# Unread f16 products on TensorE around the first and last steps of each stage of a two-layer adaLN kernel

## The chip, the cores and the metric

The program runs on one core of one Trainium2 chip. The metric is the device time of one execution in microseconds (us); the median of three runs of the kernel before is 1408.56 us. TensorE (PE in the profile, PEld for its weight loads), VectorE (DVE), ScalarE (ACT), GpSimd (POOL) and SyncE (SP, which issues the transfers) run side by side and meet at semaphores. TensorE's clock has two levels, 2.4 GHz (granted clock 1.00 in the profile) and 1.2 GHz (0.50).

## The reference

Two transformer layers over x of 32 batches x 256 tokens x 128 channels, each with a modulation computed from a condition. What is computed, cut down:

```python
mod = (_silu(L0_c) @ L0_wmod).reshape(32, 6, 1, -1)          # shifts, scales, gates
h = _layernorm(x) * (1 + ca) + sa
x = x + ga * attn0(h)      # 16 heads of 8; q, k l2-normalized; tanh resonance; sigmoid gates
h = _layernorm(x) * (1 + cb) + sb
x = x + gb * experts0(h)   # each expert picks the token with the largest logit in a group of 32
mod = (_silu(L1_c) @ L1_wmod).reshape(32, 6, 1, -1)
h = _layernorm(x) * (1 + ca) + sa
x = x + ga * attn1(h)      # 16 heads of 8; rope; softmax
h = _layernorm(x) * (1 + cb) + sb
x = x + gb * ffn1(h)       # silu(h W1) * (h W2), then two 512x512 layers with gelu, then W3
```

## The kernel before

All of x stays in SBUF. The program is a row of stages, each one an `nc.Block()` in which every engine has its own list of instructions: the set-up (line 96), attention of layer 0 (line 275), the experts (lines 779 and 932), the set-up of layer 1 (line 2254), attention of layer 1 (line 2824, which takes `attention_1_bounded` when the scores are small, as here), a short weight test `ffn_1_setup` (line 2700) and the feed-forward part `ffn_1` (line 2851). At the end of a block each engine executes a DRAIN and adds one to a gather semaphore; GpSimd collects these and sets a release semaphore, and only then does any engine enter the next block.

Inside a block the order is written out by hand. Both attention stages run `step(b, p)` for b from -3 to 32 (`every`): in four `pair`s of a step TensorE computes the scores of batch b (`scores`, line 384 or 1961) and the sums over its values (`heads`, 397 or 1975), and between them prepares the batches to come: `turn` (transposes of batch b+3, line 319 or 1913), `project_qk` (327 or 1921), `project_logits_v` (335 and 339) or `project_v` (1928), `turn_keys` and `turn_queries` (349, 359, or 1938, 1947). In steps -3 to -1 there are no scores yet, so a step is a chain: VectorE and GpSimd normalize, TensorE turns, VectorE copies, TensorE projects, and so on. ScalarE computes the exponentials or tanh of the scores (lines 473, 2046) into `probs`.

The experts stage works on chunks of 8 batches: TensorE turns (`turn`, 970), scores (978), sends tokens to slots, multiplies with the experts' matrices and hands the results back; its last work is `hand_back` (1047), after which VectorE and GpSimd add to x.

The weight test is one product (line 2704) of the largest rounding loss, read by VectorE for a flag that selects the branch of the feed-forward part. In `ffn_1` TensorE turns tile 0 (2401), then `gates(0, m)` for m = 0 to 3 (pairs of high and low parts, line 2390), `turn(1)`, and then `step(n)`, a dense stream of products of 128x512 on line 2390.

PSUM has 8 banks of 512 columns; `SC` are the four banks of the scores, `ident16` is a 128x128 unit matrix in f16 that the set-up loads.

## Time and profile before

| | us |
|---|---|
| median of 3 runs | 1408.56 (1406.98 to 1411.34) |
| the profiled execution, its own time | 1414.56 |
| its span, first to last instruction | 1412.6 |
| TensorE busy | 1258.7 (89%) |
| VectorE busy | 1066.8 (76%) |
| ScalarE busy | 926.0 (66%) |
| mean granted TensorE clock | 0.919 |

The stages in the span, by the views of the profile: set-up to 20.9 us, attention 0 to 416.1, experts to 687.4, set-up of layer 1 to 690, attention 1 to 1041.7, weight test to 1043.3, feed-forward to the end. The profile's second part cuts the span into 40 slices and gives for each the busy share of each engine and the granted clock in tenths. The timeline gives start, duration, engine, line, what is written and read, and in brackets how long the engine sat idle before and what released it.

### The profile page before, as it was taken

What the parts mean: (1) busy time and instruction counts of PE and PEld (TensorE: products, weight loads), DVE (VectorE), ACT (ScalarE), POOL (GpSimd) and SP (SyncE); (2) the same over time, 40 slices, a digit from 0 to 9 for tenths busy, and PEclk for the clock granted to TensorE, in tenths of its full rate; (3) what the DMA queues carried; (4) which work ended last, traced back from release to release, by engine and by line L of the source; (5) the groups of instructions that cost most, each with busy time, mean ns of one, the idle gap of its engine ahead of it and who ended that gap; (6) DMA issues with size and microseconds to landing.
All of it is one profiled execution on the core that took longest, in us unless ns stands there. A gap on an engine that the chain in (4) does not pass through costs nothing. (4 is left out here: it accounts for less than half of the span.)

```text
span 1412.6 us, 39634 instructions
## 1 busy us (share of the span) xinstructions
PE 1258.7 (89%) x13658; PEld 845.9 (60%) x13658; DVE 1066.8 (76%) x2966; ACT 926.0 (66%) x1280; POOL 538.4 (38%) x743
## 2 busy tenths in 40 slices
PE   2699999999977798896589999999858999999998
PEld 1455555555534677776355555555426877777876
DVE  2799999999945675743589999999835777777763
ACT  0498888888962443432078888888736666667675
POOL 1244443333412131210333343433525566566553
PEclk7599999999995897976689999999978999999999
DMA  3411111111002011100200000000000000000000
GB/s 84 154 36 35 33 35 40 36 33 33 23 10 56 23 27 27 33 2 17 91 13 13 15 11 15 13 13 15 9 2 1 9 15 15 7 15 15 7 15 24
DMA packets 44748, 37.78 MB, mean 27 GB/s; under 512 B 5008, under 2 KB 43472, under 8 KB 44144
## 3 DMA queue, kind: packets, MB, share of 16 engines
q1 hardware_dynamic: 44656, 36.56, 9.2%
q8 instruction: 57, 0.93, 0.3%
q14 instruction: 35, 0.29, 0.1%
HBM read 32.21 MB, written 4.34 MB: 26 GB/s over the span
## 5 line engine op out<-in xcount | busy, mean ns | idle before, releaser
L2046 ACT ACTIVATE a_probs<-psum_all 128x1024 f32<-128x1024 f32 x256 | 248.2, 1023 | 85.8 <-PE psum_all L1961 85.8
L473 ACT ACTIVATE probs<-psum_all,biases 128x1024 f32<-128x1024 f32 x256 | 272.7, 1113 | 39.0 <-PE psum_all L384 37.6
L2390 PE MATMUL psum_all<-ffn_hi,weights_r 128*128 128x512 f32 x704 | 285.7, 406 | 8.6 <-POOL ffn_lo L2350 5.3
L2390 PE MATMUL psum_all<-ffn_lo,weights_r 128*128 128x512 f32 x704 | 279.4, 397 | 0.0
L2350 POOL TENSOR_TENSOR ffn_lo<-ffn_full,ffn_hi 128x512 fp32r<-128x512 f32 x144 | 188.8, 1319 | 126.4 <-ACT ffn_hi L2475 86.7
L2390 PEld LDWEIGHTS psum_all<-ffn_hi,weights_r 128*128 128x128 f32 x704 | 134.1, 190 | 50.2 <-DVE ffn_full L2605 9.6
L2390 PEld LDWEIGHTS psum_all<-ffn_lo,weights_r 128*128 128x128 f32 x704 | 134.4, 191 | 26.8
L397 PE MATMUL psum_all<-probs,vpad 128*32 128x257 f32 x2048 | 139.1, 389 | 0.7 <-ACT probs L473 0.3
L1975 PE MATMUL psum_all<-a_probs,vpad 128*32 128x256 f32 x2048 | 137.8, 387 | 1.2 <-DVE a_sums L2197 1.2
L2487 ACT ACTIVATE ffn_full<-psum_all,scales 128x512 f32<-128x512 f32 x128 | 88.3, 690 | 68.5 <-PE psum_all L2390 68.3
L2350 DVE TENSOR_TENSOR ffn_lo<-ffn_full,ffn_hi 128x512 fp32r<-128x512 f32 x64 | 55.2, 863 | 79.9 <-ACT ffn_hi L2490 79.9
L496 POOL TENSOR_TENSOR a_vareps<-a_moments,eps 128x2 f32<-128x2 f32 x64 | 15.1, 236 | 201.0 <-DVE a_moments L555 201.0
L2490 ACT ACTIVATE ffn_hi<-psum_all,scales 128x512 fp32r<-128x512 f32 x128 | 87.4, 683 | 0.0
L397 PEld LDWEIGHTS psum_all<-probs,vpad 128*32 128x32 f32 x2048 | 53.7, 109 | 51.8 <-issue 21.4
L384 PE MATMUL psum_all<-a_qT,a_kT 32*128 32x256 f16 x1024 | 77.2, 276 | 8.0 <-ACT probs L473 6.3
L1975 PEld LDWEIGHTS psum_all<-a_probs,vpad 128*32 128x32 f32 x2048 | 53.6, 109 | 50.9 <-issue 27.1
L2067 POOL TENSOR_TENSOR a_vareps<-a_moments,eps 128x2 f32<-128x2 f32 x32 | 6.3, 197 | 176.6 <-DVE a_moments L2116 176.6
L1961 PE MATMUL psum_all<-a_qT,a_kT 32*128 32x256 f16 x1024 | 65.6, 276 | 4.1 <-ACT a_probs L2046 2.2
L1113 ACT COPY e_slots<-psum_all 128x512 f32<-128x512 f32 x64 | 34.4, 589 | 50.8 <-PE psum_all L992 50.7
L2475 ACT CAST ffn_hi<-ffn_full 128x512 fp32r<-128x512 f32 x64 | 39.7, 620 | 42.8 <-DVE ffn_full L2605 42.8
L1022 PE MATMUL psum_all<-e_relued,f 32*128 32x64 f32 x1024 | 50.7, 373 | 17.5 <-issue 10.6
L1151 POOL TENSOR_TENSOR X<-X,e_delta 128x256 f32<-128x256 f32 x32 | 23.6, 736 | 106.6 <-DVE e_delta L1224 106.3
(220 smaller groups left out, 2693.7 us busy)
## 6 DMA issues: line engine op xcount, KB each, us to landing
a_mod_gate<-modulation_table SPq DMA_DIRECT2D x64, 128.0 KB, 2.9
a_mod_norm<-modulation_table SPq DMA_DIRECT2D x32, 128.0 KB, 3.0
X<-in_x SPq DMA_DIRECT2D x32, 128.0 KB, 2.9
f<-in_f SPq DMA_DIRECT2D x2, 2048.0 KB, 9.8
e_mod_norm<-modulation_table SPq DMA_DIRECT2D x32, 128.0 KB, 2.9
out<-X SPq DMA_DIRECT2D x16, 256.0 KB, 2.3
e_gates<-modulation_table SPq DMA_DIRECT2D x32, 64.0 KB, 2.9
weights<-in_h SPq DMA_DIRECT2D x2, 1024.0 KB, 7.3
```

The costliest lines, as they stand in the source:

```text
L384: last = nc.tensor.matmul(SC[c % 2][:, (TT * r + kb) * T:(TT * r + kb + 1) * T], kT[p][rows, g, kb * P:(kb + 1) * P], qT[p][rows, g, :], s ...
L397: last = nc.tensor.matmul(PO[32 * r:32 * r + 32, :], vpad[p][:, kb, G * r + g, :], probs[:, (2 * g + r // 2) % 4, r % 2, kb, 0:UNIT], star ...
L473: nc.scalar.activation(probs[:, c % 4, :, :, 0:T].rearrange("p r k q -> p (r k) q"), SC[c % 2].rearrange("p (a q) -> p a q", q=T), ACT.Tan ...
L1022: last = nc.tensor.matmul(B_SLOTS[s][:, e * CG:(e + 1) * CG], f2[rows, r * EB + e, :], relued[r][rows, e, :], start=True, stop=True)
L1961: last = nc.tensor.matmul(SC[c % 2][:, (TT * r + kb) * T:(TT * r + kb + 1) * T], kT[p][rows, g, kb * P:(kb + 1) * P], qT[p][rows, g, :], s ...
L1975: last = nc.tensor.matmul(PO[32 * r:32 * r + 32, s * T:(s + 1) * T], vpad[p][:, kb, G * r + g, :], probs[:, (2 * g + r // 2) % 4, r % 2, k ...
L2046: nc.scalar.activation(probs[:, c % 4, :, :, :].rearrange("p r k q -> p (r k q)"), SC[c % 2], ACT.Exp, scale=float(np.float32(1.0) / np.sq ...
L2350: subtract(lo[layer][:, k, :], full[layer][:, k, :], hi[layer][:, k, :].bitcast(F32), ALU.subtract).then_inc(done[layer], 1)
L2390: ins = nc.tensor.matmul(dst, weights[:, w0:w0 + P], part[layer][:, k, :], start=first and i == 0, stop=last and i == len(parts) - 1)
L2475: nc.scalar.copy(hi[1][:, k, :], full[1][:, k, :]).then_inc(hi_done[1], 1)
L2487: nc.scalar.activation(full[layer + 1][:, m, :], bank[m % 2], ACT.Gelu, scale=scales[:, 1 + layer, m:m + 1]).then_inc(full_done[layer + 1], 1)
L2490: nc.scalar.activation(hi[layer + 1][:, m, :], bank[m % 2], ACT.Gelu, scale=scales[:, 1 + layer, m:m + 1]).then_inc(hi_done[layer + 1], 1)
```

## The change

A new function issues products that nobody reads, and it is called in front of, between and behind the first and last steps of the stages. The stationary operand is `ident16`, the moving one the same matrix four times, so each product streams 512 columns in f16 and writes one bank.

```diff
+def keep_busy(nc, dst, ident16, n):
+    for _ in range(n):
+        nc.tensor.matmul(dst, ident16[:, :], ident16[:, :].unsqueeze(1).broadcast_to([P, dst.shape[1] // P, P]), start=True, stop=True)
...
 # attention 0
+            def spare(b, pair):
+                places = {(-3, 3): 4, (-2, 0): 18, (-2, 3): 4, (-1, 0): 2, (-1, 1): 4, (-1, 2): 8, (B, 3): 24}
+                return places.get((b, pair), 0) if isinstance(b, int) else 0
...
                         if there(b + 3):
                             turn(b + 3)
+                    keep_busy(nc, SC[0][:, 0:512], ident16, spare(b, pair))
+            keep_busy(nc, SC[0][:, 0:512], ident16, 24)
             pe.wait_ge(wg_done, 2)
             every(pe, step)
...
 # experts, behind the last step
+            wait(pe, sent_done, B)
+            keep_busy(nc, bank[4], sbuf["ident16"], 36)
...
 # attention 1 (bounded)
+            places = {(-3, 3): 3, (-2, 0): 10, (-2, 3): 10, (-1, 1): 2, (-1, 2): 10, (B, 3): 20}
...
+                keep_busy(nc, SC[0][:, 0:512], ident16, spare(b, pair))
...
 # feed-forward
         turn(0)
+        keep_busy(nc, bank[0], sbuf["ident16"], 12)
         for m in range(KH):
             gates(0, m)
+            keep_busy(nc, bank[0], sbuf["ident16"], 2)
         turn(1)
+        keep_busy(nc, bank[0], sbuf["ident16"], 4)
...
 # weight test
             nc.tensor.matmul(psum[0:1, 0:P], worst[:, :], ident[:, :], start=True, stop=True).then_inc(moved, 1)
+            keep_busy(nc, psum[:, 512:1024], sbuf["ident16"], 16)
```

Executed are 88 such products in attention 0, 36 in the experts stage, 55 in attention 1, 16 in the weight test and 24 in the feed-forward part, 219 in all. The code inside the loops is untouched, and so are the lists of the other engines.

TensorE at the start of attention 0, before (L319 `turn`, L327 `project_qk`, L335 the logits, L339 the values, L349 `turn_keys`):

```order
L309 UNCONDITIONAL_BRANCH
L319 MATMUL psum_all<-ident,a_h 128x128 x2
L319 MATMUL psum_all<-ident,a_xn 128x128 x2
L327 MATMUL psum_all<-wqk,a_xnT 128x256 x2
L335 MATMUL psum_all<-a_wg,a_xnT 128x32 x2
```

and after (all line numbers are larger by 7):

```order
L316 UNCONDITIONAL_BRANCH
L62 MATMUL psum_all<-ident 128x512 x24
L326 MATMUL psum_all<-ident,a_h 128x128 x2
L326 MATMUL psum_all<-ident,a_xn 128x128 x2
L62 MATMUL psum_all<-ident 128x512 x4
L334 MATMUL psum_all<-wqk,a_xnT 128x256 x2
L342 MATMUL psum_all<-a_wg,a_xnT 128x32 x2
L62 MATMUL psum_all<-ident 128x512 x18
```

Nothing is moved: 24 products stand in front of the first turn, 4 between turn and projection, 18 between the first batch's logits and the second batch's turn.

TensorE at the end of attention 0 and the start of the experts, before (L397 `heads`, L408 `project_out`, L970 the experts' first turn):

```order
L408 MATMUL psum_all<-a_wo_gated,a_oT 128x128 x2
L397 MATMUL psum_all<-probs,vpad 32x257 x8
L408 MATMUL psum_all<-a_wo_gated,a_oT 128x128 x2
L275 UNCONDITIONAL_BRANCH
L957 UNCONDITIONAL_BRANCH
L970 MATMUL psum_all<-ident,e_h 128x128 x2
```

and after:

```order
L415 MATMUL psum_all<-a_wo_gated,a_oT 128x128 x2
L404 MATMUL psum_all<-probs,vpad 32x257 x8
L415 MATMUL psum_all<-a_wo_gated,a_oT 128x128 x2
L62 MATMUL psum_all<-ident 128x512 x24
L282 UNCONDITIONAL_BRANCH
L971 UNCONDITIONAL_BRANCH
L984 MATMUL psum_all<-ident,e_h 128x128 x2
```

The 24 products stand ahead of the branch that leaves the block, so ahead of the block's DRAIN. In the same way 36 stand behind the experts' last `hand_back`, 20 behind the last `project_out` of attention 1, and 16 behind the product of the weight test:

```order
L2729 MATMUL psum_all<-ident,s_worst 1x128
L62 MATMUL psum_all<-ident 128x512 x16
L2725 UNCONDITIONAL_BRANCH
L2882 UNCONDITIONAL_BRANCH
L2788 TENSOR_LOAD exact_weights
```

where before the branch followed the product of line 2704 at once.

## Rows read from the trace of the kernel before

**Rows 1.** The page's part 2, granted clock in tenths, 40 slices of 35.3 us.

```profile
PEclk7599999999995897976689999999978999999999
```

**Rows 2.** Windows: stretch, length, each engine's busy us, granted clock, DMA share, GB/s.

```profile
15.80:63.60 47.80, 20.73 (x116) 14.40 (x120) 28.39 (x118) 8.32 (x14) 13.42 (x24) 0.50 0.37 129
...
415.40:418.60 3.20, 0.06 (x1) 0.00 (x0) 1.15 (x6) 0.00 (x0) 0.86 (x2) 1.00 0.09 25
418.60:421.10 2.50, 0.00 (x0) 0.00 (x1) 1.35 (x5) 0.00 (x0) 0.04 (x1) 0.50 0.13 39
...
688.30:715.50 27.20, 12.65 (x58) 8.51 (x58) 17.48 (x51) 1.94 (x2) 8.92 (x20) 0.50 0.33 118
...
1063.80:1066.90 3.10, 0.83 (x4) 0.40 (x3) 3.03 (x6) 1.90 (x2) 1.42 (x2) 1.00 0.00 0
```

**Rows 3.** Timeline of TensorE in the lead-in of attention 0.

```profile
41.40 0.66 PE L319 MATMUL psum_all<-ident,a_h 128*128 128x128 f32 x2 [5.54 <-DVE a_xn L561]
...
43.46 2.07 PE L327 MATMUL psum_all<-wqk,a_xnT 128*128 128x256 f32 x4 [0.97 <-DVE a_xnT L597]
...
46.04 1.20 PE L339 MATMUL psum_all<-wv,a_hT 128*128 128x128 f32 x4
...
68.95 1.13 PE L327 MATMUL psum_all<-wqk,a_xnT 128*128 128x256 f32 x4
...
70.28 0.69 PE L339 MATMUL psum_all<-wv,a_hT 128*128 128x128 f32 x4
```

**Rows 4.** Timeline, products of 512 columns back to back, at either clock.

```profile
1068.86 0.63 PE L2390 MATMUL psum_all<-ffn_lo,weights_r 128*128 128x512 f32 x1
1069.29 0.63 PE L2390 MATMUL psum_all<-ffn_hi,weights_r 128*128 128x512 f32 x1
...
1086.91 0.39 PE L2390 MATMUL psum_all<-ffn_hi,weights_r 128*128 128x512 f32 x1
1087.14 0.39 PE L2390 MATMUL psum_all<-ffn_lo,weights_r 128*128 128x512 f32 x1
```

**Rows 5.** Source view, line 275 (end of attention 0): duration ns, start.

```profile
L275 PEldq DRAIN  x1: 753/753/753, 414.8 to 414.8; - x1
L275 DVEq DRAIN  x1: 459/459/459, 415.5 to 415.5; - x1
```

**Rows 6.** Timeline, the first product of the experts stage.

```profile
421.13 0.66 PE L970 MATMUL psum_all<-ident,e_h 128*128 128x128 f32 x2 [5.67 <-DVE e_h L1195]
```

**Rows 7.** Source view, line 932 (end of the experts).

```profile
L932 PEldq DRAIN  x1: 637/637/637, 685.3 to 685.3; - x1
...
L932 POOLq DRAIN  x1: 826/826/826, 686.5 to 686.5; - x1
```

**Rows 8.** Timeline, the last products of attention 1.

```profile
1037.61 0.71 PE L2001 MATMUL psum_all<-a_wo_gated,a_oT 128*128 128x128 f32 x4 [0.46 <-ACT a_oT L2040]
```

**Rows 9.** Source view, line 2824 (end of attention 1).

```profile
L2824 PEldq DRAIN  x1: 68/68/68, 1041.5 to 1041.5; - x1
```

**Rows 10.** Source view, line 2700 (end of the weight test).

```profile
L2700 PEldq DRAIN  x1: 633/633/633, 1042.1 to 1042.1; - x1
L2700 DVEq DRAIN  x1: 156/156/156, 1043.0 to 1043.0; - x1
```

**Rows 11.** Timeline of TensorE, lead-in of attention 1.

```profile
693.88 0.69 PE L1913 MATMUL psum_all<-ident,a_xhat 128*128 128x128 f32 x2 [7.96 <-DVE a_xhat L2124]
...
699.92 0.69 PE L1913 MATMUL psum_all<-ident,a_xhat 128*128 128x128 f32 x2 [2.64 <-DVE a_xhat L2124]
...
703.14 2.07 PE L1921 MATMUL psum_all<-wqk,a_hT 128*128 128x256 f32 x4 [2.53 <-DVE a_hT L2133]
```

**Rows 12.** The chain that ended last, start of the feed-forward part.

```profile
1048.08 1.13 PE psum_all L2401 x4
...
1052.18 2.06 PE psum_all L2390 x4
...
1066.83 7.81 PE psum_all L2390 x26
```

More of the change, by code:

```diff
@@ L2002, in project_out, with spare @@
             last.then_inc(projected, 1)
+        def spare(b, pair):
+            places = {(-3, 3): 3, (-2, 0): 10, (-2, 3): 10, (-1, 1): 2, (-1, 2): 10, (B, 3): 20}
+            return places.get((b, pair), 0) if isinstance(b, int) else 0
         def step(b, p):
```

## The prediction

> **What bounds the kernel now.** I read the clock first. The page grants 2.4 GHz nearly everywhere, but not at the start, in the experts stage and around the seams between stages [rows 1]; the windows give exact stretches at 0.50: 15.8 to 63.6 us and 688.3 to 715.5, the lead-ins of the two attention stages, and from 418.6 on, where the experts begin [rows 2]. What precedes the fall is idle time: TensorE ended its work in attention 0 at 415.5 [rows 5], and between 418.6 and 421.1 the clock is at 0.50 without any product in between [rows 2]. Even 2 us are enough: between 1063.8 and 1066.9 it was busy for 0.83 us, with 1.00 granted [rows 2], and the products behind it, at 1069, run at half speed again [rows 4].
>
> Then I asked what ends last in such a lead-in. It is a chain that goes round all engines: TensorE waits 5.54 us for VectorE at 41.4, 0.97 us at 43.5 [rows 3]. So a faster TensorE shortens the chain only by its own links, and unread products fit only into its waits. From 63.6 to 415.4 and in the dense part of the feed-forward stage nothing changes.
>
> Last the seams. The DRAIN that ends each engine's block spans the time until its last instruction is finished: TensorE's at the end of attention 0 took 753 ns, from 414.8 to 415.5, beside the 0.7 us of the last projection, and VectorE's ended at 416.0 [rows 5]. TensorE's was 637 ns at the end of the experts [rows 7] and 633 ns behind the one product of the weight test [rows 10]. The whole core enters the next block only after the last DRAIN. That is what decides this case, since four of the added groups stand ahead of a DRAIN.
>
> **Price of one product.** No f16 product of 512 columns is in the trace. The nearest are those of line 2390 with 512 columns: 0.43 us from start to start at the low clock, 0.23 at the high one [rows 4]. I take these. Those are products of a wider type that reload their weights each time, so an f16 one can hardly be slower; as bounds I allow half of the price at the high clock and 0.43 throughout.
>
> The Trainium skill ("TensorE: Matmul & The Clock Gate", Back-to-back issue gap) gives about 131 ns per product of 512 columns in a sustained stream of weight loads and products. The rows show 230 ns for such pairs; by the page the groups at the seams would be cheap, a rival below.
>
> **The seams, which cost.** Each end is compared with the engine that was last.
> - End of attention 0: 24 x 0.23 = 5.5 us behind 415.5 gives 421.0; VectorE was done at 416.0 [rows 5]. +5.0. The clock is high there [rows 2].
> - End of the experts: 36 x 0.23 = 8.3 behind 686.0 gives 694.3; GpSimd was last, at 687.3 [rows 7]. +6.9 at the high clock. In the last third of the experts the clock swings [rows 1]; at the low one until it rises 8 to 16 products cost 0.2 more each, +8.5 to +10.
> - End of attention 1: the last projection ended at 1038.3 [rows 8], yet TensorE's DRAIN came at 1041.5 [rows 9], so over 3 us pass in the jump across the other branch's code. 20 x 0.23 = 4.6 behind 1038.3 gives 1042.9. If the jump overlaps them, +1.4; if it begins after them, +4.6. The instructions are issued ahead of their execution (the DRAIN of the weight test starts with its product, at 1042.1 [rows 10]), so I take nearer the lower end: +2.0.
> - Weight test: 16 x 0.23 = 3.7 behind 1042.7 gives 1046.4, VectorE was done at 1043.2 [rows 10]. +3.2; at the low clock, which is possible after the gap in the seam before, +6.6.
>
> Sum: 5.0 + 6.9 + 2.0 + 3.2 = +17.1 us, from 16.5 (the jump overlapped) to 26.
>
> Do they buy the next stage a high clock? No. What follows the release is again idle TensorE: the experts' first turn came at 421.1 [rows 6], 5.1 us after VectorE's DRAIN; attention 1's at 693.9 [rows 11], 6.6 after GpSimd's; the feed-forward's at 1048.1 [rows 12], 4.9 after VectorE's. These distances stay, because the chain starts at the release. The clock fell after 3.1 us at most [rows 2, 5], so each stage starts at 0.50 as before, and the groups at the seams are pure cost.
>
> **The lead-ins, which gain.**
> - Attention 0. The 24 products in front start at the block's entry, 20.9 us: at most 24 x 0.43 = 10.3, so done by 31.2, when the first turn begins, and earlier since such a dense run raises the clock (products at line 2390 went from 0.43 to 0.23 in the same way). The 18 cost 4.1 at the high clock and 7.7 at the low, against a wait of 5.54; the groups of 4 take 0.92 against a wait of 0.97 [rows 3], and those of 2, 4 and 8 behind the second batch stand in like waits. With the clock up, projection, logits and values take 68.95 to 70.97 instead of 43.46 to 47.24 [rows 3]: 1.8 us less for the second batch and for the third, 1.1 for the first, which has no values. Three turns save 0.45 each (half their streaming), and the first scores and sums until 63.6 another 1.2. Sum 7.2 us. VectorE is busy for 28.4 of the 47.8 us there [rows 2] and is next in the chain when TensorE is early; I let it take back a third: -4.9 (from -7 to +1, if the clock falls again in the wait before the turn and the 18 run slow).
> - Attention 1. The stage starts at 0.50. 3 slow products behind the first turn cost 1.3 us, 0.5 over their wait; the 10 behind the projection fit into 2.64 us only once the clock is up, the next 10 into 2.53 [rows 11]; VectorE has about 2 us of other work before it needs that turn. From the second projection on the clock is up: 2.07 becomes 1.13 and 1.06 becomes 0.69 (as the like products in [rows 3]), with the wait between them twice 1.1 us, and 0.7 for turns and scores; against it 0.3 for the 3. Sum -2.6 (from -3.5 to 0).
> - Feed-forward. Idle before the first turn, so 12 products at 0.50: 5.2 us in a wait of 3.0 (from 1049.2 to 1052.2) [rows 12], +2.2 if the clock stays down, +1.3 if it rises on the way; then the first gates take about 1.1 instead of 2.06, -0.9. The middle is a chain of ScalarE and VectorE, in which the groups of 2 and 4 hide. The dense part began at the low clock, 26 products in 7.81 us [rows 12] instead of 26 x 0.23 = 6.0, -1.7 if it now begins high. Sum -0.9 at best, +1.5 at worst; I take -0.6.
>
> **Sum.** +17.1 - 4.9 - 2.6 - 0.6 = +9.0 us. On the profiled execution, span 1412.6, that is a span of 1421.6 (its own time 1414.56 would be 1423.6); on the median of the runs, 1408.56, it is **1417.6**.
>
> **Rivals.**
> - The seams don't hold: a DRAIN lets the products run on behind it. Then the groups at the seams cost nothing, they fill the waits up to the next first turn almost exactly (5.7 us of idle against 5.5 [rows 6]; 7.96 against 8.3 [rows 11]), and every stage starts at the high clock. Against it: three DRAINs that ended with their last product [rows 5, 7, 10]. The 17.1 go, the experts' first steps gain perhaps 2, attention 1 and the feed-forward another 2: 1408.56 - 8.1 - 4 = 1396.5. Chance 0.08. This is the faster side.
> - The products are cheap, about 0.13 us, near the page's rate and half that of [rows 4]. Seams 2.6 + 3.4 + 0 + 1.6 = 7.6, lead-ins -8.1: 1408. The condition is that the narrow type streams at half the distance of [rows 4]; for it stands nothing in the trace, where 512 columns take the same 0.23 in every pair. Chance 0.04. Beside it: the lead-ins give their full 7 + 3.5 + 1 and the jump overlaps: +16.5 - 11.5 = +5 and less, 1409 to 1412.8. Chance 0.09.
> - The lead-ins gain nothing, because the waits that are left between the groups let the clock fall again and slow products then overrun their waits: +17.1 + 0 to 2, 1425.7 to 1428. Its place is the wait that is left of some 2 us between the 24 or the 18 and the next turn; 2 us sufficed once [rows 2]. Chance 0.08.
> - The experts end, or the weight test begins, at the low clock: 3.4 more for one, up to 7 for both, 1421 to 1425. Chance 0.13.
>
> **How the numbers follow.** Forecast 0.58 (1413 to 1421), rivals 0.08, 0.13, 0.08, 0.13. The range 1410.5 to 1427 leaves out the faster rival and the outermost of two others. A measurement of this kernel can tell about 0.3%, 4.2 us, from no change: faster 0.08, same 0.13, slower 0.79.
>
> **What would show it.** TensorE's DRAIN at the four seams long (5.5, 8.3, over 1 and 3.7 us) and last; the distance from a release to a stage's first turn unchanged; the clock at 0.50 at the experts' and at attention 1's first turn, but at 1.00 from about 28 us on in the lead-in of attention 0; the first tanh of line 473 some 3 us earlier within its stage, and that of the fifth some 5. I am wrong if VectorE starts the experts' statistics at 417 while TensorE still runs the 24, or if the unread products stand less than 0.2 us apart.

## The result, and the profile after

The changed kernel takes 1425.09 us (median of 14 runs, 1421.82 to 1429.8), the kernel before, beside it, 1410.96 us (14 runs, 1403.31 to 1421.27). The ratio is 1.0086 (95%: 1.0067 to 1.0105), which on 1410.96 is 12.1 us slower, from 9.5 to 14.8; the medians are 14.1 apart. The profiled execution has a span of 1422.3 us, against 1412.6. The forecast was 1417.6 us in a range of 1410.5 to 1427, slower. The direction and the range held, and so did the mechanism at the ends of the stages; what the forecast said of the feed-forward part and of the experts did not. The forecast itself was 7.5 us under the median, and 2.4 of that lie in the kernel before, whose median was 1410.96 in these runs and not 1408.56. In the experiments below three runs of the kernel before took 1861 to 3798 us; the ratios leave them out, and its medians move by at most 0.5 us with them.

First the ends of the stages. Source views of the lines of the four blocks in the profile after (engine, duration in ns, start in us):

```profile
L282 DVEq DRAIN  x1: 459/459/459, 410.1 to 410.1; - x1
L282 PEldq DRAIN  x1: 4050/4050/4050, 411.2 to 411.2; - x1
...
L946 POOLq DRAIN  x1: 826/826/826, 686.7 to 686.7; - x1
L946 PEldq DRAIN  x1: 4048/4048/4048, 690.0 to 690.0; - x1
...
L2850 DVEq DRAIN  x1: 54/54/54, 1045.8 to 1045.8; - x1
L2850 PEldq DRAIN  x1: 502/502/502, 1046.7 to 1046.7; - x1
...
L2725 DVEq DRAIN  x1: 156/156/156, 1048.4 to 1048.4; - x1
L2725 PEldq DRAIN  x1: 1907/1907/1907, 1049.7 to 1049.7; - x1
```

In [rows 5, 7, 10] TensorE's DRAIN took 0.6 to 0.75 us and was over before VectorE's or GpSimd's. Now it is the last one in each of the four blocks (at the end of attention 1 it was the last before too, by 0.2 us). The timeline of TensorE shows what it waits for (start, duration, operation, in brackets the idle time before):

```profile
409.30 0.71 PE L415 MATMUL psum_all<-a_wo_gated,a_oT 128*128 128x128 f32 x4 [0.61 <-DVE a_oT L723]
409.85 5.34 PE L62 MATMUL psum_all<-ident 128*128 128x512 f16 x24
420.36 0.66 PE L984 MATMUL psum_all<-ident,e_h 128*128 128x128 f32 x2 [5.16 <-DVE e_h L1211]
...
686.05 7.94 PE L62 MATMUL psum_all<-ident 128*128 128x512 f16 x36
700.57 0.69 PE L1929 MATMUL psum_all<-ident,a_xhat 128*128 128x128 f32 x2 [6.57 <-DVE a_xhat L2146]
...
1042.66 4.48 PE L62 MATMUL psum_all<-ident 128*128 128x512 f16 x20
...
1047.97 3.63 PE L62 MATMUL psum_all<-ident 128*128 128x512 f16 x16
1056.52 1.12 PE L2423 MATMUL psum_all<-ident,ffn_xhat 128*128 128x128 f32 x4 [4.92 <-DVE ffn_xhat L2601]
```

The DRAIN at 411.2 ends at 415.2, and so do the 24 products (409.85 + 5.34 = 415.2). The next stage's first turn comes 5.15 us behind that, as it came 5.1 us behind VectorE's DRAIN in [rows 5, 6]. The same holds at attention 1 (6.55 us, as in [rows 7, 11]) and in the feed-forward part (4.90, as in [rows 10, 12]). The products delay the release, and what follows the release stays as it was, the idle TensorE with it.

The clock, by windows (stretch, length, busy us of PE, PEld, DVE, ACT and POOL with counts, granted clock, DMA share, GB/s):

```profile
30.30:33.60 3.30, 3.30 (x10) 2.10 (x8) 1.51 (x7) 0.00 (x0) 0.90 (x2) 0.50 0.00 0
23.60:30.10 6.50, 3.58 (x19) 1.58 (x17) 2.18 (x12) 0.00 (x0) 3.26 (x6) 1.00 0.34 100
...
415.50:418.90 3.40, 0.00 (x0) 0.00 (x0) 0.73 (x5) 0.00 (x0) 0.90 (x2) 1.00 0.13 39
419.40:421.50 2.10, 0.68 (x3) 0.31 (x3) 1.42 (x8) 0.37 (x1) 0.32 (x2) 0.50 0.21 62
699.28:706.11 6.83, 5.54 (x14) 2.98 (x15) 3.58 (x11) 0.00 (x0) 2.55 (x4) 0.50 0.91 317
...
1074.80:1081.50 6.70, 5.95 (x14) 4.72 (x15) 2.05 (x11) 3.10 (x5) 4.35 (x5) 0.50 0.00 0
```

In the lead-in of attention 0 the clock is at 1.00 from 23.6 us on, but for 3.4 us about 32, where it was at 0.50 until 63.6 [rows 2]. It is still at 1.00 right behind the seam (415.5 to 418.9, TensorE idle) and at 0.50 when the experts' first turn comes. In attention 1 it is at 0.50 for 6.8 us in place of 27 [rows 2]. In the feed-forward part it fell again at the start of the dense stream (last row).

### The profile page after: what moved, and what is told of

Read it like the earlier page. It is cut to its first block and busy times, and to the rows that moved or that the text cites. A ratio compares the mean times of both kernels' runs of the same rounds, so it can differ in the third digit from the quotient of the medians.

```text
span 1422.3 us, 40072 instructions
## 1 busy us (share of the span) xinstructions
PE 1285.7 (90%) x13877; PEld 849.9 (60%) x13877; DVE 1067.6 (75%) x2966; ACT 926.0 (65%) x1280; POOL 538.6 (38%) x743
## 5 line engine op out<-in xcount | busy, mean ns | idle before, releaser
L62 PE MATMUL psum_all<-ident 128*128 128x512 f16 x219 | 57.1, 413 | 7.3 <-PEq L103 7.3
## 6 DMA issues: line engine op xcount, KB each, us to landing
f<-in_f SPq DMA_DIRECT2D x2, 2048.0 KB, 10.5
```

The costliest lines, as they stand in the source:

```text
L62: nc.tensor.matmul(dst, ident16[:, :], ident16[:, :].unsqueeze(1).broadcast_to([P, dst.shape[1] // P, P]), start=True, stop=True)
```

## Where the time went, stage by stage

Each stage can be cut at its DRAINs, since they stand in every profile: a stage runs from the release to the DRAIN of the engine that was last before (VectorE's, in the experts stage GpSimd's), a seam from there to the next release. Worked out in this way from the start and the duration of the DRAINs in the two traces, in us:

| part | before | after | change | forecast |
|---|---|---|---|---|
| attention 0, entry to VectorE's DRAIN | 395.2 | 391.1 | -4.2 | -4.9 |
| seam behind it | 0.56 | 5.25 | +4.7 | +5.0 |
| experts | 270.8 | 271.8 | +1.0 | 0 |
| seam, with the set-up of layer 1 | 2.8 | 9.3 | +6.5 | +6.9 |
| attention 1, release to VectorE's DRAIN | 351.2 | 349.0 | -2.2 | -2.6 |
| seam behind it | 0.5 | 1.6 | +1.1 | +2.0 |
| weight test | 1.35 | 4.2 | +2.9 | +3.2 |
| feed-forward | 369.2 | 370.4 | +1.2 | -0.6 |

With 1.3 us less in the set-up, which the change doesn't touch, these make the 9.7 us between the two spans. How steady such a length is, the profiles of the experiments below show: attention 0 took 394.2 to 395.3 us in four kernels without its lead-in products and 390.0 to 391.1 in nine with them, attention 1 351.2 to 352.9 in four without (one more left out, below) and 349.0 to 352.0 in nine with them. The experts stage is not steady: the same code took 263.0 to 274.1 us in nine profiles. This is why the experiments are read by stages, and by medians where the experts stage is meant.

## Experiments

**1. The seams and the lead-ins apart.** Two kernels, each with one half of the change.

```diff
 # lead-ins alone (lead_only), against the changed kernel
-                places = {..., (-1, 2): 8, (B, 3): 24}
+                places = {..., (-1, 2): 8, (B, 3): 0}
...
-            wait(pe, sent_done, B)
-            keep_busy(nc, bank[4], sbuf["ident16"], 36)
...
-            places = {..., (-1, 2): 10, (B, 3): 20}
+            places = {..., (-1, 2): 10, (B, 3): 0}
...
-            keep_busy(nc, psum[:, 512:1024], sbuf["ident16"], 16)
```

> The changed kernel without its four groups ahead of a stage's end (24, 36, 20 and 16 products); the products inside the lead-ins stay. Theory (the DRAIN holds the core until the unread products have ended; 4.7 + 6.5 + 1.1 + 3.1 = 15.3 us by the trace of after): 15 us less than the changed kernel, so 5 us under the kernel before (ratio 0.996, from 0.993 to 0.999): attention 0 shorter by 4, attention 1 by 2, the feed-forward part longer by 1. TensorE's DRAINs end before VectorE's or GpSimd's, as in the kernel before. Rival (the loss has another cause, such as the feed-forward's start or the clock in the experts stage): less than 8 us of the loss goes, ratio to before 1.000 to 1.006.

Measured: 1405.03 us (12 runs) against 1411.71 of before, ratio 0.9958 (0.9931 to 0.9985). Attention 0 391.1, attention 1 350.8, feed-forward 370.0. The loss of the change hangs on the four groups: the change turns from slower to faster when they go. By the ratios that is 18 us, 3 more than the 15.3 of the seams (see experiment 6).

> The four groups ahead of the stages' ends alone (24, 36, 20, 16), nothing in the lead-ins. Theory: each group costs what it overlaps nobody's work by: 4.7 + 6.5 + 1.1 + 3.1 = 15.3 us over the kernel before (ratio 1.011, 1.009 to 1.013); the next stages still begin at 0.50. Rival (part of the cost comes back because the next stage begins sooner at the high clock): 1.006 or less.

The other half: 1427.0 us (4 runs), 15.3 us over the median of before, as worked out; ratio 1.010 (1.0055 to 1.0145), which is 14 us, from 8 to 20. The seams are 5.25, 9.25, 1.6 and 4.2 us long, to 0.03 us those of the changed kernel, and the feed-forward part takes 368.8.

**2. The seams doubled.** The four groups with 48, 72, 40 and 32 products.

```diff
 # seams_twice, against seams_only
-                places = {(B, 3): 24}
+                places = {(B, 3): 48}
...
-            keep_busy(nc, bank[4], sbuf["ident16"], 36)
+            keep_busy(nc, bank[4], sbuf["ident16"], 72)
...
-            places = {(B, 3): 20}
+            places = {(B, 3): 40}
...
-            keep_busy(nc, psum[:, 512:1024], sbuf["ident16"], 16)
+            keep_busy(nc, psum[:, 512:1024], sbuf["ident16"], 32)
```

> The four groups doubled (48, 72, 40, 32), nothing in the lead-ins. Theory: 96 more products at 0.216 us each, all behind the engine that was last: 20.7 us over the run with the single groups, so 36 us over the kernel before (ratio 1.0255, 1.023 to 1.029). Rival (products are cheap and the single groups' cost is a fixed one of the DRAIN): within 5 us of the run with the single groups. Rival (a long group raises the clock at the next stage's start and pays part back): 10 to 15 us over it.

Measured: 1444.12 us (6 runs), ratio 1.0221 (1.018 to 1.0262), a little under the expected 1.023 to 1.029; by the medians 17 us over the single groups and not 20.7. The four seams themselves are 20.6 us longer in the profile; what gave some of that back over the whole kernel is open, but for 1.3 us in the feed-forward part (experiment 5). The profiled execution, 1454.9, is one of two in six that were some 10 us longer. Attention 1 took 358.0 us in it; I read its seams and its last stage only. Source view of lines 282 and 945 (the ends of attention 0 and of the experts):

```profile
L282 DVEq DRAIN  x1: 461/461/461, 415.2 to 415.2; - x1
L282 PEldq DRAIN  x1: 4050/4050/4050, 421.5 to 421.5; - x1
...
L945 PEldq DRAIN  x1: 4048/4048/4048, 706.9 to 706.9; - x1
```

Its timeline of TensorE:

```profile
415.00 10.52 PE L62 MATMUL psum_all<-ident 128*128 128x512 f16 x48
430.89 0.66 PE L983 MATMUL psum_all<-ident,e_h 128*128 128x128 f32 x2 [5.37 <-DVE e_h L1210]
...
695.22 15.71 PE L62 MATMUL psum_all<-ident 128*128 128x512 f16 x72
...
1068.49 8.80 PE L62 MATMUL psum_all<-ident 128*128 128x512 f16 x40
...
1078.11 7.08 PE L62 MATMUL psum_all<-ident 128*128 128x512 f16 x32
```

Between 24 and 48 products lie 5.18 us, between 36 and 72 7.77: 0.216 us each. The seam behind attention 0 is 10.43 us: the 10.52 of the group, less the 0.67 by which it begins ahead of the end of VectorE's DRAIN (415.67), plus the 0.58 from the last product to the next release. A rival that makes the products cheap is out, and one that makes the cost a fixed one of the DRAIN too.

**3. The groups behind the release.** The groups of the seams are taken away, and others stand at the front of the next list: 22 in the experts stage, 10 in the set-up of layer 1, 10 in attention 1, 16 in the feed-forward part. These are 58 products and not the same number as the 96 of the seams, as the expectation has it.

```diff
 # moved, against lead_only
+            keep_busy(nc, bank[4], sbuf["ident16"], 22)
             wait(pe, w_loaded, 16 * len(dram["experts_loads"]))
...
+        keep_busy(nc, SC[0][:, 0:512], ident16, 10)
+
         def step(b, p):
...
+        @block.tensor
+        def _(pe):
+            keep_busy(nc, psum[:, 0:512], sbuf["ident16"], 10)
...
+        keep_busy(nc, bank[0], sbuf["ident16"], 16)
         turn(0)
```

> The same number of unread products, but the four groups stand behind the release of the next stage: 22 at the front of the experts' list, 10 in the set-up of layer 1, 10 in front of attention 1, 16 in front of the feed-forward part, in place of 24, 36, 20 and 16 ahead of the DRAINs. Theory (place, not number, makes the cost): no DRAIN is held, and the idle 5 to 7 us behind each release are filled, so that the experts, attention 1 and the feed-forward part begin with the clock at 1.00. At least as good as the lead-ins alone: 5 to 11 us under the kernel before (0.992 to 0.997). Rival (products cost what they stream wherever they stand): no better than the changed kernel, 1.006 to 1.010. Second rival (the first turns come from VectorE's chain, and a high clock is worth nothing there): equal to the lead-ins alone within 1 us.

Measured: 1413.19 us (12 runs), ratio 1.0011 (0.9986 to 1.0037): against the kernel before in the same session it is 1.5 us up, where the change is 14.1 up, and the lead-ins alone are 6.7 down. No DRAIN is held now but one, so the first half of the theory stands. Its second half failed, since the kernel is no better than the lead-ins alone. Neither rival fits either: it is faster than the changed kernel, and 8 us slower than the lead-ins alone. Timeline of TensorE at the experts' start and at the feed-forward's:

```profile
411.22 4.91 PE L62 MATMUL psum_all<-ident 128*128 128x512 f16 x22 [1.36 <-PEq L793]
415.97 0.38 PE L984 MATMUL psum_all<-ident,e_h 128*128 128x128 f32 x2
...
422.41 0.66 PE L979 MATMUL psum_all<-ident,e_takenT 128*128 128x128 f32 x2 [4.47 <-DVE e_takenT L1224]
...
1042.40 6.38 PE L62 MATMUL psum_all<-ident 128*128 128x512 f16 x16 [1.75 <-PEq L2731]
1048.62 0.60 PE L2428 MATMUL psum_all<-ident,ffn_xhat 128*128 128x128 f32 x4
```

The experts' first turn was at the high clock (0.38 us in place of the 0.66 of [rows 6]). Yet the second came 11.5 us behind the release, where it came 11.1 behind in the profile of before: VectorE and ScalarE set the pace there, and in the 4.47 us of idle time the clock fell again. In the feed-forward part the 16 ran half slow and ended at 1048.6, 7.5 us behind the weight test, where the turn had come at 4.9; that stage took 371.8. The 10 in the set-up took 4.0 us at the low clock and held its DRAIN by 1.5. So at the experts a start at the high clock is worth next to nothing, and a group costs where it overruns its wait. Most of the 8 us lie elsewhere, in the rest of the experts stage (experiment 6).

**4. Which lead-ins pay.** First the two of attention alone, with nothing in the feed-forward part; then the kernel before with only the 24 in front of attention 0.

```diff
 # a0_a1, against lead_only
-        keep_busy(nc, bank[0], sbuf["ident16"], 12)
         for m in range(KH):
             gates(0, m)
-            keep_busy(nc, bank[0], sbuf["ident16"], 2)
         turn(1)
-        keep_busy(nc, bank[0], sbuf["ident16"], 4)
...
 # a0_front, against before
+            keep_busy(nc, SC[0][:, 0:512], ident16, 24)
             pe.wait_ge(wg_done, 2)
             every(pe, step)
```

> Only the unread products in the lead-ins of the two attention stages (24 in front and 4, 18, 4, 2, 4, 8 between in attention 0; 3, 10, 10, 2, 10 in attention 1); nothing at a stage's end and nothing in the feed-forward part. Theory: attention 0 from its entry to VectorE's DRAIN 391.1 us instead of 395.2 (-4.1), attention 1 350 instead of 351.5 to 353 (about -2), the feed-forward part back at 368.8 to 369.3 from 370.0: 6 to 7 us under the kernel before, ratio 0.995 (0.992 to 0.998), 1 us better than all lead-ins together. Rival (the products in the feed-forward's start cost nothing, the 1 us there is scatter of one profile): the feed-forward part stays at 370.

> The kernel before plus the 24 products in front of attention 0 alone; the 40 between its first steps are left out. Stage length from entry to VectorE's DRAIN: 395.2 us before, 391.1 with all 64. Theory (the clock must be held through the waits of 5.5 and some 3 us that follow): it falls again behind the first turn, so that at most the first turn and projection gain, 394 to 395. Rival (the 24 wake the clock and the chain's own work holds it): 391 to 392, and the 40 are for nothing.

Measured: a0_a1 1404.86 us (8 runs) against 1412.34, which is 7.5 us less; ratio 0.9917 (0.9885 to 0.9949), which is 12 us less. So far apart are the two measures where runs scatter. Attention 0 390.0, feed-forward 369.3. In eight profiles without products at its start the feed-forward part takes 368.8 to 369.3 us (leaving out that of seams_twice, for which see experiment 5), in the two with them 370.0 and 370.4. So they cost 1.1 us; too little to be seen in the medians, clear by stages.

In attention 1 the profiles with lead-in products fall into two groups. In the changed kernel and in that of experiment 3 the clock stays up behind its first rise, and the stage takes 349.0 and 349.3 us. In the other seven it falls once more for 3.4 us, and the stage takes 350.8 to 352.0. The window of that fall in lead_only:

```profile
703.90:707.30 3.40, 3.40 (x20) 2.41 (x22) 1.73 (x9) 1.11 (x2) 1.46 (x3) 0.50 0.00 0
```

Without such products the same holds: 351.2 us without a second fall, in the kernel before, and 352.6 to 352.9 with one, in three others. Like with like, the products gain 2.1 us or 1.1. What decides on the second fall isn't shown.

The kernel with the 24 alone took 1405.95 us in its one run, but its experts stage, which the edit leaves alone, was 263.0 us, the shortest of nine. The 24 left attention 0 at 394.4 us, within what kernels without them have (394.2 to 395.3). Windows of that kernel:

```profile
24.00:30.60 6.60, 3.83 (x19) 1.69 (x17) 2.00 (x10) 0.00 (x0) 3.25 (x6) 1.00 0.35 97
30.80:61.40 30.60, 18.98 (x105) 13.30 (x106) 22.00 (x83) 7.75 (x13) 10.09 (x18) 0.50 0.45 165
```

and its timeline of TensorE:

```profile
30.02 0.41 PE L326 MATMUL psum_all<-ident,a_h 128*128 128x128 f32 x2 [2.77 <-DVE a_xn L575]
...
39.86 0.66 PE L326 MATMUL psum_all<-ident,a_h 128*128 128x128 f32 x2 [5.48 <-DVE a_xn L575]
```

They wake the clock, and it falls behind the 2.77 us of idle time and stays down until 61.4. Without the 40 products between the steps the gain of 4 us is gone. Whether they would reach it without the 24 in front was not run.

**5. The dense start of the feed-forward part.** a0_a1 with 8 products ahead of the second of the four pairs that make up the first product of the dense part.

```diff
+                if isinstance(n, int) and n == 0 and (layer, m, k) == (1, 0, 1):
+                    keep_busy(nc, bank[1], sbuf["ident16"], 8)
                 if m == 0:
                     value_ready(layer, n, k)
```

> The kernel of the run with the two attention lead-ins, plus 8 unread products in the one wait of 2.03 us between the first pair and the rest of the first product of the feed-forward's dense part, into a bank that is free until then. Theory: what cost 0.2 us for each of 8 to 14 products was the clock that fell in that wait; filled, it stays at 1.00 and the feed-forward part gets 1.5 to 2.5 us shorter than in that run (366.5 to 367.5 against 369). Whole: 0.994. Rival (behind a chain at its own pace ScalarE and VectorE are next, the dense part is led by them for its first tile): less than 0.5 us. Second rival (at that place the clock is at 0.50 already, so the 8 take 3.4 us and overrun the wait by 1.4): up to 1 us longer.

The expectation has the wait of 2.03 us behind the first pair. In the traces it stands behind the third, in the changed kernel and in a0_a1:

```profile
1075.56 0.77 PE L2412 MATMUL psum_all<-ffn_hi,weights_r 128*128 128x512 f32 x1 [2.03 <-POOL ffn_lo L2372]
...
1059.65 0.66 PE L2410 MATMUL psum_all<-ffn_hi,weights_r 128*128 128x512 f32 x1 [2.03 <-POOL ffn_lo L2370]
```

The 8 products therefore push the second and the third pair into that wait.

Measured: the feed-forward part takes 367.4 us, 1.9 less. A window over the dense start:

```profile
1063.00:1075.00 12.00, 9.96 (x46) 7.62 (x44) 7.51 (x22) 8.29 (x13) 6.36 (x6) 1.00 0.00 1
```

and the timeline of TensorE:

```profile
1061.27 2.25 PE L62 MATMUL psum_all<-ident 128*128 128x512 f16 x8
1063.17 0.58 PE L2410 MATMUL psum_all<-ffn_hi,weights_r 128*128 128x512 f32 x1
...
1065.29 0.47 PE L2410 MATMUL psum_all<-ffn_hi,weights_r 128*128 128x512 f32 x1 [0.84 <-POOL ffn_lo L2370]
```

The clock was at 0.50 when the 8 began, yet they took 2.25 us and not 3.4: it rose under them. The fourth pair comes 23.7 us behind the release in both kernels, so all of the 1.9 us are gained behind it. In experiment 2 the clock rose in that wait by itself, and the feed-forward part took 367.5 us there, with nothing added, 1.3 less than with the single groups. So the clock at the dense start is worth 1.3 to 1.9 us, about the 1.7 that the forecast had for it. As a whole this kernel is at 1404.4 us, ratio 0.9937 (0.991 to 0.9963), not apart from a0_a1: its profile has the experts stage at 274.1 us.

**6. What stays over.** The stages explain 10 us of the change, the ratio says 12.1, the medians 14. With the groups moved, 7 of the 8 us between its profile and that of the lead-ins alone lie in the experts stage. Two kernels with the lead-ins of a0_a1 and one group at the experts' entry, and one with that group alone:

```diff
 # leads_front: a0_a1, and experts_front: before, each with
+            keep_busy(nc, bank[4], sbuf["ident16"], 22)
             wait(pe, w_loaded, 16 * len(dram["experts_loads"]))
...
 # leads_end24: a0_a1 with
-                places = {..., (-1, 2): 8, (B, 3): 0}
+                places = {..., (-1, 2): 8, (B, 3): 24}
```

> The kernel before plus one group: 22 unread products at the front of the experts' list, behind the release, in the 5 us in which TensorE waits there. The profile of the run with all groups moved behind the releases had the experts stage at 274.9 us, against 267.7 to 271.8 in five other profiles. Theory (the start at the high clock is worth nothing, since VectorE's chain sets the first turns, and the 3 to 7 us are scatter of where the clock falls later in this stage): same as before, ratio 0.998 to 1.002, the second turn 11.1 to 11.5 us behind the release as before. Rival (the group at the front makes the clock fall at worse places later): 3 to 7 us slower, 1.002 to 1.005. Second rival (it buys the experts' first steps): 2 us faster or more.

> Both attention lead-ins plus the 22 products at the front of the experts' list. Over the medians, the changed kernel and the one with all groups moved are some 5 us slower than their stages outside the experts explain, all others are not. Theory (scatter of where the clock falls in the experts stage, no cause in the change): as the two parts apart, 0.9917 and 0.9966, so 0.990 to 0.995. Rival (the warm lead-in of attention 0 together with products at the experts' entry makes the experts stage longer): 0.997 to 1.000.

> Both attention lead-ins plus the 24 products ahead of the DRAIN of attention 0. Theory: 4.7 us over the run with the two lead-ins alone, which is ratio 0.996 (0.993 to 0.999), all of it between VectorE's DRAIN and the release of the experts. Rival (the same interaction with the experts stage): 9 to 10 us over it, 0.999 to 1.001.

Measured: the group alone 1409.05 us, ratio 0.9966 (0.9945 to 0.9987); with the lead-ins 1412.05, 0.9985 (0.9959 to 1.0011); with the 24 ahead of the DRAIN 1415.38, 1.002 (0.9996 to 1.0044), which is 10.5 us over a0_a1 where the seam is 4.7. The sessions differ, but their runs of before agree (1412.34 and 1412.23). The group alone was expected to change nothing, and the kernel came out 3 us faster. The theory of mere scatter missed there and in the two others: by the medians, products at the experts' entry cost 6 to 10 us more than by themselves once the lead-ins are there (+7.2 against -3.3 for the group of 22, +10.5 against the seam's 4.7 for the 24). Windows over the experts stage, and over 52 us in its middle, of leads_front:

```profile
410.89:689.62 278.73, 223.90 (x3612) 176.59 (x3612) 155.66 (x479) 97.83 (x177) 52.47 (x96) 0.80 0.09 25
...
510.90:562.90 52.00, 44.83 (x793) 36.43 (x794) 29.48 (x89) 20.36 (x37) 8.32 (x16) 0.77 0.12 29
```

and of a0_a1:

```profile
411.03:679.66 268.63, 212.13 (x3590) 168.60 (x3590) 155.49 (x479) 97.77 (x177) 52.33 (x96) 0.82 0.10 25
...
511.00:563.00 52.00, 44.53 (x869) 35.67 (x868) 35.79 (x114) 22.68 (x41) 13.07 (x24) 0.93 0.13 30
```

Over the stage VectorE, ScalarE and GpSimd do the same work in the same busy time in both; only TensorE's differs, with the clock. In the middle of the stage the longer one had a granted clock of 0.77 where the other had 0.93, and did 76 fewer products in 52 us. Why a group at the entry should move the clock's falls 100 us later isn't settled, and its size is uncertain too, since profiles of one code scatter by as much.

**7. Products where the clock falls in the experts stage.** In each chunk it falls in the four rounds of `second_matrices` (64 small products each) and stays low for 7 to 31 us in a0_a1. That kernel with 1, 5, 2 and 5 unread products ahead of these rounds, in a bank that is free there:

```diff
             def second_matrices(m, r, sends):
+                wait(pe, inner_done, (m + 1) * ROUNDS)
+                keep_busy(nc, bank[2], sbuf["ident16"], (1, 5, 2, 5)[r])
                 wait(pe, relued_done, m * ROUNDS + (r + 1))
```

> Both attention lead-ins plus unread products inside the experts stage, 1, 5, 2 and 5 ahead of the four rounds of the second matrices in each of the four chunks of 8 batches, where TensorE waits 0.5, 1.2, 0.6 and 1.2 us; 52 products, 11 us of streaming. In each chunk the clock falls in these rounds and stays at 0.50 for some 20 us, in which a round takes 3.7 us instead of 2.0. Theory (waits filled keep the clock, and the experts stage is led by TensorE there): up to 5 us less in each chunk, 10 to 20 us in all, ratio 0.980 to 0.985, the clock at 1.00 from the third step to the end of the stage. Rival (the clock falls all the same, since what brings it down is not the waits but the small products themselves, 32 partitions x 64 columns): no gain, and 0 to 8 us lost where the slow products overrun their waits: 0.992 to 0.998.

Measured: 1388.73 us (6 runs, 1382.9 to 1390.4) against 1412.23, ratio 0.9829 (0.9802 to 0.9855). Timeline of TensorE in a0_a1, two of the rounds of the third chunk:

```profile
584.94 3.40 PE L1036 MATMUL psum_all<-e_relued,f 32*128 32x64 f32 x64 [1.23 <-issue]
...
589.94 3.69 PE L1036 MATMUL psum_all<-e_relued,f 32*128 32x64 f32 x64 [0.55 <-DVE e_slots L1101]
```

and of the filled kernel:

```profile
579.94 1.25 PE L62 MATMUL psum_all<-ident 128*128 128x512 f16 x5
581.24 2.01 PE L1038 MATMUL psum_all<-e_relued,f 32*128 32x64 f32 x64
...
590.43 2.01 PE L1038 MATMUL psum_all<-e_relued,f 32*128 32x64 f32 x64
```

and the window over its experts stage:

```profile
411.49:662.36 250.87, 203.12 (x3642) 152.08 (x3642) 155.18 (x479) 97.47 (x177) 52.25 (x96) 0.92 0.11 27
```

The 5 products take the 1.2 us in which TensorE waited anyway, and the round then takes 2.01 us instead of 3.4 to 3.7. The experts stage went from 268.6 to 250.9 us at a clock of 0.92 instead of 0.82; in the last chunk the clock was still low for 17 us. Its six runs lie within 8 us, the 23 of before in the same session within 14. That doesn't show that the scatter went with the clock of this stage, since the 14 runs of the changed kernel lie within 8 as well.

**8. Together.** The last kernel is that of experiment 7 with the 8 products of experiment 5 and more of them in the experts' last chunk, whose waits are longer:

```diff
-                keep_busy(nc, bank[2], sbuf["ident16"], (1, 5, 2, 5)[r])
+                keep_busy(nc, bank[2], sbuf["ident16"], ((1, 5, 2, 5) if m < NCHUNK - 1 else (9, 5, 6, 5))[r])
...
+                if (m, r) == (NCHUNK - 1, 3):
+                    keep_busy(nc, bank[2], sbuf["ident16"], 5)
```

> The kernel of the run with fill in the experts stage (1388.7 us), plus the 8 products in the wait of the feed-forward's dense start, plus more fill in the last chunk of the experts, whose waits are longer there (9, 5, 6, 5 ahead of the four rounds in place of 1, 5, 2, 5, and 5 behind the last), where the clock was at 0.50 for 17 us still. Theory: feed-forward part 367.4 instead of 368.9 (-1.5), last chunk held at 1.00 (-3 to -5, for rounds of 3.2 and 3.7 us and turns of 3.8 become 2.0 and 2.2): 1382 to 1385, ratio 0.979 to 0.981. Rival (in the last chunk VectorE and ScalarE are the ones waited for, so a fast TensorE only waits longer): the experts stage stays at 250 to 251 us, 1387.

Measured: 1380.09 us (5 runs) against 1410.31, ratio 0.9781 (0.9754 to 0.9808), 2 us under the expected 1382 to 1385. The experts stage takes 246.8 us, 4.0 less, and the feed-forward part 367.4. It is the fastest of all, 30 us under the kernel before, with the same kind of products that cost 12 us in the change. The granted clock over 40 slices, of the changed kernel:

```profile
PEclk8999999999989997785999999999999999999999
```

and of this one; the experts are the 13th to the 20th slice, 9 9 9 7 7 8 5 9 above and 6 9 9 9 9 9 9 8 here, so that the low digit left stands at the stage's first steps:

```profile
PEclk8999999999996999999899999999969999999999
```

## The prediction, point by point

- **A DRAIN waits for unread products: right.** Shown by four DRAINs that end with the last product, by the doubled groups and by the kernel without the groups. The rival of products that run on is out.
- **Price of a product, 0.23 us: close.** 0.216 from the doubled groups. At the seams of attention 0 and the experts that is 0.3 and 0.4 us less than forecast. The rate of about 131 ns (the Trainium skill, "TensorE: Matmul & The Clock Gate", Back-to-back issue gap) was not seen for this shape.
- **End of attention 1, +2.0: too high, +1.1 measured.** The step that failed is the jump across the other branch's code: I took nearer the lower end of "overlapped" and "not", and it is overlapped in full. TensorE's DRAIN ended at 1047.16, with the 20 products (1042.66 + 4.48).
- **The next stages still start at the low clock: right.** Their first turns took 0.66, 0.69 and 1.12 us, as before, and came 5.15, 6.55 and 4.90 us behind the release, as before. The clock fell within that idle time. Experiment 3 adds what the forecast lacked: with its first turn at the high clock the experts' second turn came no earlier.
- **Lead-in of attention 0, -4.9: right, -4.2 measured.** The first tanh came 2.2 us earlier in its stage and the fifth 4.9 (some 3 and 5 were forecast), so 0.7 of the gain is lost again behind the fifth. If the 7.2 us of the shorter links are right, the chain takes two fifths back and not one third; which engine does wasn't shown. The clock did fall once behind the wait ahead of the first turn, as the rival with no gain had it, but came back in 3.4 us, under the 4 products and the projection. With the 40 products taken away it stayed down, and the gain was gone (experiment 4). With "at 1.00 from about 28 us on" the forecast left that fall out.
- **Lead-in of attention 1, -2.6: about right, -2.2** between the two profiles; over all profiles the gain is nearer 1.3 (means of 352.4 and 351.1), and it hangs on whether the clock falls a second time (experiment 4).
- **Feed-forward, -0.6: wrong in sign, +1.2.** One term failed, the -1.7 for a dense part that begins at the high clock. It rested on the groups of 2 and 4 holding the clock. The last of them stands ahead of two waits, 0.98 and 2.03 us long (0.24 and 2.03 before), and the clock fell there: 14 slow products in place of 8, and the stage from the fourth pair on (the product at 1075.56 in experiment 5) took 346.5 us in place of 345.6. The wait of 2 us that had been my own evidence for how little suffices [rows 2, 4] stood at just this place. The other term, 12 products ahead of faster gates, came out as the forecast had it at its better end (+1.3 - 0.9): the gates came 5.13 us behind the turn in place of 4.10, but the fourth pair stands 23.9 us behind the release in place of 23.7, so 0.3 of that was left. In lead_only 0.8 was left, and the dense part took no longer than before. Experiment 5 shows the 1.7 us to be there once the clock is up.
- **Experts, 0: undersized.** I priced only the stage's start. By the profile it is +1.0; by the runs it is 2 to 4, what the 12.1 to 14.1 us leave beside the 10 of the other parts, and with one group at the experts' entry 6 to 10 by the medians of experiment 6. I had seen in [rows 1] that the clock swings in this stage, and drew from it a price for the seam only, not for the stage. Why lead-ins and products at the entry together make this stage longer stays open.
- **How near the sum came is in part luck.** The four seams came out 1.9 us under the 17.1, the four stages together 3.9 over the -8.1, and these errors have opposite signs. The median of 1425.09 lies outside the 1413 to 1421 that had 0.58 of the chances, between the bands of two rivals, neither of which happened: the groups of the experts and the weight test ran at the high clock (7.94 us for 36, 3.63 for 16), and the lead-ins of attention did gain. By the ratio, on the 1408.56 of the forecast, it would be 1420.7.
- **Sums.** The bounds of the feed-forward term are -1.3 and +1.3 by its own parts and not -0.9 and +1.5. The weight test's group at the low clock makes +6.4 and not +6.6, and +5 on 1408.56 is 1413.6 and not 1412.8. None of these changes the forecast.

## What to carry over

Put filler work only where an engine waits for another within a stage, and not ahead of a barrier at which TensorE arrives last: there every product counts in full, since the barrier waits for the last one. Where other work hides them they cost less, like the 20 at the end of attention 1, 4.5 us long, which cost 1.1. Size each group by the wait that it fills at the clock that holds there, and look for the place where the clock falls and long work follows, not for the stage's edge: 52 products in the rounds of the experts gained 16 us by the medians (12 by the ratios), 24 alone in front of attention 0 nothing in that stage. Compare stages between fixed marks, since the whole time can scatter by more than the effect.

## What the hardware showed that I had not expected

- TensorE's DRAIN behind a long group lasts 4.05 us whether 24, 36, 48 or 72 products stand ahead of it (4050, 4048, 4050, 4048 ns). At 0.216 us each it begins some 19 products ahead of their end, by estimate the distance by which the issue runs ahead. Behind the 16 of the weight test it lasts 1.91 us. Where the jump to the end of attention 1 lies between, it was 0.50 and 0.67 us with 20 and 40 products.
- In the experts stage the clock falls while TensorE is busy with products of 32 partitions x 64 columns, between waits of 0.5 to 1.2 us; 13 products of 512 columns per chunk in these waits kept it up in most of the stage.
- In the eleven profiles in which TensorE idled some 5 us at the experts' entry, the clock fell there, with 5 or 10 us of products right ahead of that wait as without them.
